# Causal attention layers with paired heads, copies ahead of low halves, one run of value products, and paired statistics

## The reference

```python
# layer 1, after the softmax; one mean and variance for each head of an image
attn = jax.nn.softmax(mixed, axis=-1)
mean = jnp.mean(attn, axis=(2, 3), keepdims=True)
var = jnp.var(attn, axis=(2, 3), keepdims=True)
attn = (attn - mean) * jax.lax.rsqrt(var + EPS)
# layers 2 and 3
att = jnp.einsum('bqhd,bkhd->bhqk', q, k) * scale
causal = jnp.tril(jnp.ones((t, t), dtype=bool))
att = jnp.where(causal[None, None], att, jnp.finfo(att.dtype).min)
att = jax.nn.softmax(att, axis=-1)
out = jnp.einsum('bhqk,bkhd->bqhd', att, v).reshape(b, t, c)
```

## Time and profile before

| what | value |
|---|---|
| median of three runs | 831.8 us (831.14 to 832.46) |
| the profiled execution: its time / its span | 834.57 us / 832.4 us |
| mean granted clock of PE (1 is 2.4 GHz) | 0.962 |
| PE busy | 763.8 us, 92% |
| DVE busy | 593.8 us, 71% |
| ACT busy | 576.5 us, 69% |
| POOL busy | 257.8 us, 31% |
| layer 1 | about 82 to 262 us |
| layer 2, causal attention | about 298 to 448 us |
| layer 3, causal attention | about 523 to 670 us |

### The profile page before, as it was taken

The page is one execution under the profiler, slowest core; times in us unless marked ns, Lnnn a source line. Parts: engine busy times, 40 slices in busy tenths (PEclk is TensorE's granted clock), DMA queues, the critical chain, the costliest instruction groups (busy, mean ns, idle before and its releaser), DMA issues.

```text
span 832.4 us, 17775 instructions
## 1 busy us (share of the span) xinstructions
PE 763.8 (92%) x5481; PEld 586.9 (71%) x5481; DVE 593.8 (71%) x1534; ACT 576.5 (69%) x1431; POOL 257.8 (31%) x505
## 2 busy tenths in 40 slices
PE   1997999999998989999998875999999978999997
PEld 1965877788786857777775674677777676777775
DVE  6146777777776667888875986678788716787775
ACT  2324878778777567878876754788888626877785
POOL 1802355656563441212111000222121201433334
PEclk9998999999999999999999985999999968999999
DMA  6000001011111223333321003223333203222320
GB/s 210 1 1 1 1 11 20 12 20 20 20 17 20 58 73 87 99 91 85 100 80 39 1 1 76 78 78 102 85 89 100 76 1 79 48 48 68 75 48 20
DMA packets 63271, 44.48 MB, mean 53 GB/s; under 512 B 34416, under 2 KB 55280, under 8 KB 63088
## 3 DMA queue, kind: packets, MB, share of 16 engines
q1 hardware_dynamic: 63216, 43.78, 21.1%
HBM read 12.24 MB, written 3.21 MB: 19 GB/s over the span
## 4 chain that ended last, share of the span: by engine, by line
PE 79%; DVE 12%; ACT 3%; issue 3%; POOL 1%; DMA 1%; POOLq 0%; SPq 0%; DVEq 0%
PE ps L1201 13%; PE ps L961 9%; PE ps L1366 8%; PE ps L1355 8%; PE ps L1064 6%; PE ps L968 5%; PE ps L972 4%; PE ps L992 3%; PE ps L1048 3%; PE ps L993 3%; PE ps L1006 3%; PE ps L1036 2%; PE ps L911 2%; PE ps L1015 1%; PE ps L1340 1%
## 5 line engine op out<-in xcount | busy, mean ns | idle before, releaser
L603 ACT ACTIVATE ee<-ps,nmax 128x128 f32<-128x128 f32 (+1 forms) x584 | 207.5, 444 | 8.5 <-DVE nmax L1534 5.1
L1201 PE MATMUL ps<-w,ee 128*128 128x128 f32 x960 | 140.6, 275 | 4.0 <-ACT big L590 1.5
L1201 PEld LDWEIGHTS ps<-w,ee 128*128 128x128 f32 x960 | 113.1, 143 | 21.0 <-ACT ee L603 7.2
L1537 DVE TENSOR_REDUCE nmax<-ps 128x2 f32<-128x256 f32 x200 | 101.8, 551 | 24.5 <-PE ps L972 23.6
L590 ACT ACTIVATE big<-ps 128x512 f32<-128x512 f32 (+1 forms) x192 | 97.6, 552 | 31.2 <-PE ps L1201 30.4
L1882 DVE TENSOR_TENSOR hhl<-ee,hhl 128x512 fp32r<-128x512 f32 x96 | 79.8, 837 | 31.2 <-ACT hhl L832 29.4
L961 PE MATMUL ps<-kh,big 128*128 128x256 f32 x384 | 94.7, 391 | 1.7 <-POOL big L364 1.2
L1534 DVE TENSOR_REDUCE nmax<-ps 128x4 f32<-128x1024 f32 x48 | 58.7, 1224 | 38.9 <-PE ps L961 38.4
L507 POOL TENSOR_TENSOR xc<-big,xc 96x512 f32<-96x512 f32 x32 | 53.0, 1657 | 107.5 <-DVE big L1876 107.3
L1355 PE MATMUL ps<-qk,w1hl 128*128 128x512 f32 x288 | 85.2, 407 | 0.4 <-DVE ee L1885 0.4
L1366 PE MATMUL ps<-hhl,w2hl 128*96 128x512 f32 x288 | 83.1, 399 | 0.3 <-DVE hhl L1882 0.3
(11 more groups left out here) (264 smaller groups left out, 1352.5 us busy)
## 6 DMA issues: line engine op xcount, KB each, us to landing
qk<-hl SPq DMA_DIRECT2D x288, 96.0 KB, 3.1
big<-moe_gate SPq DMA_DIRECT2D x8, 768.0 KB, 6.9
w<-w_in SPq DMA_DIRECT2D x1, 1735.0 KB, 13.3
xc<-x_in SPq DMA_DIRECT2D x4, 384.0 KB, 6.2
l_mix<-on SPq DMA_DIRECT2D x32, 48.0 KB, 2.1
tok<-l_mix SPq DMA_DIRECT2D x16, 96.0 KB, 2.0
out<-xc SPq DMA_DIRECT2D x8, 192.0 KB, 2.1
w<-w_in SPq DMA_DIRECT2D x1, 998.0 KB, 9.8
```

The lines of the kernel that those rows point to most:

```text
L603: last = nc.scalar.activation(ee[:, ke, hh, qc, 0:w], src, ACT.Exp, bias=nmax[:, kp, hh, qc:qc + 1])
L1201: last = nc.tensor.transpose(ps[:, 4 + hh, b * P:(b + 1) * P], ee[:, u, hh, qc, tc * P:(tc + 1) * P], ident)
L1537: last = V.tensor_reduce(out=nmax[:, kp, :, qc], in_=ps[:, 2 * kp:2 * kp + 2, qc * N:qc * N + scores_cols(l, qc)], axis=AX.X, op=ALU.max, ...
```

## The change

Five things are changed, four of them in the causal layers.

**Paired heads.** Each `qk` slot now holds both heads of a pair in all 128 rows, and where a query half is the stationary operand, the moving one has the other head's rows at zero. One product with 2 x 256 columns and one with 2 x 128 take the place of four; the long one (query half 1) comes first. PSUM banks now belong to query halves, and the masks are one product for each. The weights are laid out by slots on the host (`by_slot`), so that the scaling of queries takes eight small DVE operations.

**One run of value products.** `weigh_values(0)` leaves the end of unit 2 and stands in the next unit 0 directly ahead of `weigh_values(1)`, behind the waits for `et0`, `et1`, `oc` and `v_sb`. The same holds at the layer's end.

**Copies ahead of low halves.** In DVE's unit 0 the order is `copy_probs(0)`, `copy_probs(1)`, `keys`.

**Last two images written out.** The loops run to image 13, and images 14 and 15 follow without the work for images that don't exist.

**Paired statistics in layer 1.** Two batch norm instructions of 512 elements take the place of four of 256. They read the two heads alternately, so that even places are one head and odd places the other, and POOL needs one operation less, on half as many elements.

```diff
--- before.py
+++ after.py
@@ score_unit, PE
                 else:
-                    for qc in range(TPI):
-                        w = scores_cols(l, qc)
-                        for hh in range(2):
-                            r0 = hh * 4 * HD
-                            mm(ps[:, 2 * kp + hh, qc * N:qc * N + w], qk[r0:r0 + 4 * HD, par, u, 0, qc * P:(qc + 1) * P],
-                               qk[r0:r0 + 4 * HD, par, u, 1, 0:w], start=(qc == 0), stop=False)
-                    for hh in range(2):
-                        diag = ps[:, 2 * kp + hh, :].rearrange("p (b t) -> p b t", t=P)[:, 0::3, :]
-                        last = mm(diag, identb[:, :], mid_dim(maskb[:, :], 1, TPI), start=False, stop=True)
+                    for qc in reversed(range(TPI)):
+                        w = scores_cols(l, qc)
+                        mm(both(kp, qc, w), qk[:, par, 3 + u, qc * P:(qc + 1) * P], qk[:, par, u::6, 0:w], start=True, stop=False)
+                    for qc in range(TPI):
+                        w = scores_cols(l, qc)
+                        last = mm(both(kp, qc, w)[:, :, w - P:w], identb[:, :], mid_dim(maskb[:, :], 1, 2), start=False, stop=True)
@@ new helpers
+        def before(n, end):
+            return not isinstance(n, int) or n < end
+        def both(kp, qc, w):
+            return ps[:, 2 * kp + qc, 0:2 * w].rearrange("p (h t) -> p h t", h=2)
@@ unit, PE
+                        if l == 3 or not isinstance(i, int) or i > 0:
+                            pe.wait_ge(*upto(l, "oc", i))
+                            pe.wait_ge(*upto(l, "v_sb", i))
+                        weigh_values(l, npar, 0)
                         weigh_values(l, npar, 1).then_inc(own(l, "av"), 1)
...
-                        project_qk(l, i + 2, par)
+                        if before(i + 2, B):
+                            project_qk(l, i + 2, par)
...
-                    if l > 1 and u == 2:
-
-                        pe.wait_ge(*upto(l, "oc", i + 1))
-                        pe.wait_ge(*upto(l, "v_sb", i + 1))
-                        weigh_values(l, par, 0)
@@ unit, DVE
                     if l > 1 and u == 0:
                         copy_probs(0)
-                        keys(l, i + 2, par, i // 2 + 1 if isinstance(i, int) else it + 1)
                         copy_probs(1)
+                        if before(i + 2, B):
+                            keys(l, i + 2, par, i // 2 + 1 if isinstance(i, int) else it + 1)
...
-                        for hh in range(2):
-                            for q in range(TPI):
-                                last = V.bn_stats(est[:, par, q, 2 * u + hh, :], ee[:, u, hh, q, :])
+                        for q in range(TPI):
+                            last = V.bn_stats(est[:, par, q, u, :], ee[:, u, :, q, :].rearrange("p h t -> p t h"))
@@ start of layer 1, DVE
-                    V.tensor_scalar(wa("l2_q"), wa("l2_q"), QS, None, ALU.mult).then_inc(sg("l2_wq"), 1)
-                    V.tensor_scalar(wa("l3_q"), wa("l3_q"), QS, None, ALU.mult).then_inc(sg("l3_wq"), 1)
+                    for name in ("l2", "l3"):
+                        for a, side, lo, hi in ((0, 0, 2, 3), (0, 1, 0, 2), (1, 0, 1, 3), (1, 1, 0, 1)):
+                            v = wa(f"{name}_qk{a}").rearrange("p (s d u) -> p s d u", s=2, u=3)[:, side, :, lo:hi]
+                            V.tensor_scalar(v, v, QS, None, ALU.mult).then_inc(sg(f"{name}_wq"), 1)
@@ loops, alike on PE, ACT, DVE, POOL and SP
-                    with pe.Fori(1, B // 2) as it:
+                    with pe.Fori(1, B // 2 - 1) as it:
                         for j in range(6):
                             unit(j, it * 6 + j, it * 2 + j // 3)
+                    for j in range(6):
+                        unit(j, 3 * B - 6 + j, B - 2 + j // 3)
```

More of the change, by code:

```diff
@@ L477, in _ @@
                             normed_image(l, i - 2, par)
+                    for par in range(2):
+                        normed_image(l, B - 4 + par, par)
                     normed_image(l, B - 2, 0)
@@ L991, in project_qk @@
                     pe.wait_ge(sg("l1_var"), n - 4)
-                mm(ps[0:C, 7, 0:N], wa(f"l{l}_q"), x, start=True, stop=True)
-                mm(ps[0:C, 7, N:2 * N], wa(f"l{l}_k"), x, start=True, stop=True).then_inc(own(l, "q_ps"), 1)
+                first, second = ("l1_q", "l1_k") if l == 1 else (f"l{l}_qk0", f"l{l}_qk1")
+                mm(ps[0:C, 7, 0:N], wa(first), x, start=True, stop=True)
+                mm(ps[0:C, 7, N:2 * N], wa(second), x, start=True, stop=True).then_inc(own(l, "q_ps"), 1)
             def parts_ready(l, n):
@@ L1174, in unit @@
                     npar = 1 - par
[L1175 removed]
+                    if before(k + 2, 3 * B):
                         if u == 1:
@@ L1193, in unit @@
                         if l > 1 and u == 2 and hh == 1:
-                            pe.wait_ge(*upto(l, "v_sb", i + 2))
+                            if before(i + 1, B):
+                                pe.wait_ge(*upto(l, "v_sb", i + 2))
                             if not isinstance(i, int) or i >= 2:
@@ L1536, in maxima @@
                     for qc in range(TPI):
-                        last = V.tensor_reduce(out=nmax[:, kp, :, qc], in_=ps[:, 2 * kp:2 * kp + 2, qc * N:qc * N + scores_cols(l, qc)],
+                        last = V.tensor_reduce(out=nmax[:, kp, :, qc], in_=both(kp, qc, scores_cols(l, qc)),
                                                axis=AX.X, op=ALU.max, negate=True)
@@ L1733, in _ @@
                 if l > 1:
-                    with dve.Fori(1, B // 2) as it:
+                    with dve.Fori(1, B // 2 - 1) as it:
                         for j in range(6):
                             unit(j, it * 6 + j, it * 2 + j // 3)
+                    for j in range(6):
+                        unit(j, 3 * B - 6 + j, B - 2 + j // 3)
                 if l > 1:
```

98 lines of the change are left out of this document (53 added, 45 removed).

## The result

The changed kernel takes 824.22 us (median of seven runs, 821.46 to 826.67), the kernel before beside it 832.46 (831.14 to 833.95): a ratio of 0.9901 with a 95% interval of 0.9876 to 0.9926. It is faster by 8.2 us where 16.0 were forecast, and 824.2 lies 1.2 above the range.

The account below looks back on a forecast made before the run. PE was taken to bound the kernel. 32 images x 0.45 = 14.4, last images 4.8, ends of layers -1.3, start of layer 3 -0.65, layer 1 -1.2: total 16.0, so 831.8 - 16.0 = 815.8 us, range 808.5 to 823.

Parts of the forecast that it names:

- The image: Layers 2 and 3: each image 0.45 us shorter, 0.20 if waits bite, 0.70 if not; 32 images give 14.4.
- PE alone: One causal image without waits: three score units at 0.16 each plus the stall of 0.25, 0.73 us less.
- the price of unit 0: Unit 0 of an image: score unit 0.58 us instead of 0.74; L992 starts at 2.22 instead of 2.31.
- The place of the value run: Unit 0: value products wait for ACT's last copy of probabilities, starting at 0.67 us; only 0.09 of 0.16 arrives.
- The layers' ends: Moved value run: 0.67 us a layer lost at the end, 0.65 at layer 3's start, hidden at layer 2's.
- hidden by 0.5 us: Stack transfers on SP's queue: landed by 357.5, with the score unit that reads them at about 358.0.
- Copies ahead: DVE's unit 0, both copies before the low halves: PE's stall of 0.25 us at the second three transposes goes.
- Last images: Images 14 and 15 of each causal layer: 1.03 and 1.35 us saved, 2.4 a layer, 4.8 in all.
- Start of layer 1: Six more small DVE operations behind the held L1652: 0.5 us lost, up to 0.8, or up to 1.5 won.
- Statistics: Layer 1, paired statistics reading elements 2 KB apart: 0.7 us lost, from 0.5 won to 3 lost.
- The rival that gave 823.8: Causal layers: DVE's and ACT's chain sets the image, 0.20 us less each; chance 0.15.
- my three signs of being wrong: Image period outside 8.0 to 8.5, tails saving under 1 us a layer, or DVE reaching 11.8 in layer 1's middle image.

Follow-up runs that it names:

- the short copies: Changed kernel with DVE's two copies of unit 0 bringing only 128 of 384 columns, so work is left out: 817.45 us, ratio 0.9818.
- the split: Changed kernel with the first run of value products back at the end of unit 2, the second still in the next unit 0: 819.75 us, ratio 0.986.
- the short product first: Changed kernel with the 256-column score product ahead of the 512-column one: 823.22 us, ratio 0.9873.
- the loops: Changed kernel with the loops running to the last image again, including work for images that don't exist: 827.68 us, ratio 0.9939.
- single statistics: Changed kernel with four statistics instructions of 256 elements a unit again and POOL's longer sum of squares: 822.52 us, ratio 0.9856.
- scaling later: Changed kernel with the eight small scaling operations moved from the start of layer 1 into images 4 and 6: 823.79 us, ratio 0.9871.

## Why the prediction was wrong

**The image, forecast 0.45 less, measured 0.31.** This is the term that failed: 32 x 0.14 = 4.5 of the 7.8 us that are missing. PE alone was to give 0.73, and I let waits take 0.28 of it: 0.07 ahead of the value run, 0.06 for `ob`, 0.15 in the third unit. The small waits for DVE's run came out at that size: 0.22, shown by the short copies, in which they vanish. The step that failed is the price of unit 0. I had the score unit there at 0.58 like the two others, and the stretch from the transposes to L1002 at 2.22 instead of the old 2.31. Measured it takes 2.31 and 2.37 in turn, so nothing is won there. After the change its score unit takes 0.61 + 0.24 because it stands for ACT's exponentials, and the joined run's 0.12 (0.06 in every second image) pays for a part of that. In the split order, where nothing holds it, it still takes 0.55 + 0.23. By PE's own times the stretch would be 0.35 + 0.23 + 1.55 = 2.13, so either order loses about 0.20; 0.73 - 0.20 - 0.22 = 0.31. The rows could have told the 0.55 only by bounds: my upper bound of a score unit was 0.67, from the masks, and I gave none for the product's place behind other forms. The masks themselves fell to 0.23, as forecast with the saved change of form. The drain at a change of tiling mode that I named beside this stands in the Trainium skill, page "TensorEngine Tiling (Array Packing)", section "Key Properties", and not in the section that I gave; the 0.23 agrees with it, but no run isolates it.

**The place of the value run.** I forecast a wait for ACT's copy of probabilities ahead of the value products. It isn't there: the copy ends at 353.16 + 0.49 = 353.65, and the value products begin at 354.01, behind the masks. What came is a wait for ACT's exponentials ahead of the score unit, which needs their PSUM banks back: the run that was moved had covered this too, and I had not read what the first instruction that moves forward waits for. In steady state it costs no more than the joined product's 0.55 does in the other order, 2.31 and 2.37 in turn against 2.34. So the merge is neither gain nor loss there. That joining itself gives nothing was forecast; that two losses cancel is luck.

**The layers' ends.** I forecast 0.67 a layer lost by the moved run at the end, and 0.65 at the start of layer 3 alone; the split wins 2.1 and 1.3. About 0.8 of the 2.1 is a wait that I had called hidden by 0.5 us: in image 14 of layer 2 PE stands for the last stack transfer. The rest is 0.7 at the end, as forecast, and 0.7 at the start (24.9 to the third L1002 against 24.2), which I had called hidden in layer 2. PE's timeline of after, where nothing is projected any more between the transposes and this unit, and the time to landing in that stretch, where the median is as before:

```profile
424.70 0.61 PE L978 MATMUL ps<-qk 128*128 128x512 f32 x2 [0.98 <-DMA qk<-hl]
```

```profile
DMA to landing us min/median/max: 3.1/3.2/4.3
```

The slow one took 4.3, in both traces of the changed kernel; in the split kernel the maximum is 3.2 and PE doesn't wait. The joined run isn't the cause: the kernel with the short product first has that run too, and its transfers land in at most 3.3 there, so PE doesn't wait. From the twelfth L1002 of layer 2 to the feed-forward that kernel takes 47.7 us, the changed one 48.5, the split one 47.0. The change from loop to written-out code falls here, with two instruction transfers in the same stretch of every kernel, but that these delayed it was not tried and stays open. My slack was also worked out for an image that projects: image 14 comes to the unit a microsecond earlier.

**Copies ahead.** Right in mechanism and size: 0.23 alone of the forecast 0.25, and 8.8 us of time. Its partner is the surprise: paired heads alone bring 0.12 an image and nothing in the time. With a stall on DVE ahead, a faster PE waits longer; I had put both into one sum of PE times, which holds only if both are made.

**Last images.** Forecast 2.4 a layer, measured 2.0 and about 1.1. In layer 2 the stack wait is in the 2.0: the kernel with the short product first, without it, is 2.5 shorter than the loops from the twelfth projection on (47.7 against 50.2). **Start of layer 1.** Forecast 0.5 lost; the chain's product behind group norm begins at 79.01 instead of 77.72: 1.3. The small operations are not what costs: they are over 3.79 us after the first began, the two large ones were after 3.66. But before, four group norm statistics ran beside the held L1652 and were over with it, at 70.55:

```profile
67.58 2.97 DVE L1402 BATCH_NORM_STATS2 chst<-xc 96x6 f32<-96x256 f32 x4
```

After the change they begin only at 70.55 and take 1.33. I had not read what ran in the shadow of the held operation. **Statistics.** Forecast 0.7 lost, 1.3 to 1.9 won: an instruction of 512 elements that alternate between places 2 KB apart takes 0.69 us, as my price without any penalty had it (0.67).

```profile
L1721 DVE BATCH_NORM_STATS2 est<-ee x20: 677/695/708, 176.3 to 212.0; 128x6 f32<-128x512 f32 x20
```

The rule of the Trainium skill that I set beside it, a penalty for each other line (page "Advanced Engine Details and Errata", section "Memory Cachelines") doesn't show here; the extra 0.75 ns of the gate comparisons was no measure for this instruction. The Trainium skill's rule that products in different row groups run side by side (page "TensorE: Matmul & The Clock Gate", section "Part 3: Packing small matmuls — row/col tiling") didn't make the old form the better one in units 1 and 2: the joined products take 0.38 and 0.35 there, the old ones 0.42. In unit 0 of the split order they take 0.55.

**The sum, with measured terms:** 32 x 0.31 = 9.9; last images 2.0 and 1.1; the moved run at the layers' ends and starts, without the stack wait, -1.3 and about -1.0; layer 1 between 0 and +0.6. That is 10.7 to 11.3, between the 8.2 of the medians and the 13.2 of the profiles. A part of the rest is the start of layer 2, where 24.9 us to the third projection stand against 22.8 before. The split explains 0.7 of these 2.1. The stretch also moves with the granted clock of 298 to 327, 23.3 us at 0.95 (single statistics) and 26.5 at 0.88 (scaling later), but what sets both was not tried. What else is missing I place, without a run that shows it, in other stages where PE is granted the lower clock for a part of the time. Windows of after:

```profile
298.00:327.00 29.00, 26.25 (x221) 19.28 (x220) 20.08 (x53) 21.70 (x61) 7.96 (x10) 0.94 0.28 77
...
510.00:530.00 20.00, 18.17 (x145) 13.12 (x146) 12.62 (x35) 13.38 (x36) 1.89 (x3) 0.91 0.20 53
```

Before, the same stretches had 0.99 and 0.66, but they hold other work: layer 3's first score unit stands at 513.3 before and at 507.2 after. At the same distance from it, 516.1 to 536.1, the clock before was 0.81. I can't assign this to a part of the change, and leave it open.

The rival that gave 823.8 (DVE and ACT set the image, 0.20 each) had the right time, but in part by luck: the image gained 0.31, which is 3.5 us more over the layers than it had, and other stages took that back. Its mechanism is half of what is seen: DVE's run and ACT's exponentials do hold PE, but with DVE's run shortened and no wait left the image is still 0.20 above my price. None of my three signs of being wrong came: the image is within 8.0 to 8.5, the last images save over 1 us, and DVE is busy for 8.5 us in a middle image of layer 1.

## What to carry to other kernels

When PE work is made cheaper, ask first which engine ends the next wait: the order of two DVE instructions was worth 8.8 us, the cheaper products alone nothing that the time shows. Price a matmul by rows in which it stands in the place that it will have, with the same products and waits ahead, not by a stretch of its like. Before moving a block away from another, list the waits that the block covered, those of the instruction that now comes first too. Before splitting an operation that stands held, look for work that runs in its shadow.

## What was not expected of the hardware

The two fp32r products of a score unit over all rows take 0.35 to 0.38 us behind products with 96 or 128 output rows in units 1 and 2, and 0.55 behind products with 32 output rows, with no wait named between; the four row-halved ones took 0.42 to 0.43 in both places. Whether the form ahead or a weight load that isn't early makes the difference stays open. Batch norm statistics over alternating places 2 KB apart ran at 0.69 us for 512 elements, close to the 0.67 that contiguous ones of 96 and 256 elements lead one to expect. Eight scaling operations of 16 to 32 columns stood 3.8 us beside POOL's work up to the end of a memset, where the batch norm statistics put in their place were not held. And runs of one kernel lay 5 us apart with the mean granted clock between 0.954 and 0.965.
